# A routed two-layer network on one core: TensorE's products of a turn in another order, the shared weights' split in halves, and weight loads that wait by a table

## The reference

```
gates = xf @ rW + rb
topk_vals, topk_idx = jax.lax.top_k(gates, TOP_K)          # TOP_K = 2 of 8 experts
h = _gelu(jnp.einsum('td,edh->eth', xf, W1) + b1[:, None, :])   # 1024 -> 256
y = jnp.einsum('eth,ehd->etd', h, W2) + b2[:, None, :]          # 256 -> 1024
moe = jnp.einsum('te,etd->td', w, y)
return (shared + moe).reshape(B, L, D)
```

## Time and profile before

| | us |
|---|---|
| median of 3 runs (333.43 to 336.17) | 335.24 |
| the profiled execution, its own time | 334.91 |
| its span, first to last instruction | 333.0 |
| TensorE products busy | 317.9 (95%) |
| TensorE weight loads busy | 274.6 (82%) |
| VectorE busy | 241.2 (72%) |
| ScalarE busy | 188.3 (57%) |
| the loop, from the end of turn 1 to its last product | about 194 to 297.6 |

### The profile page before, as it was taken

One profiled execution on the slowest core, in us unless ns is written; L12 is line 12 of the kernel. 1 busy time (PEld: TensorE's weight loads), 2 busy tenths in 40 slices (PEclk: granted clock), 3 DMA queues, 4 the chain that ended last, 5 costly groups with the idle time before them and its releaser, 6 DMA issues.

```text
span 333.0 us, 6122 instructions
## 1 busy us (share of the span) xinstructions
PE 317.9 (95%) x1994; PEld 274.6 (82%) x1994; DVE 241.2 (72%) x466; ACT 188.3 (57%) x315; POOL 80.2 (24%) x94
## 2 busy tenths in 40 slices
PE   6999999999999999999999999999999999999994
PEld 2889897787799888879989887897788878878874
DVE  2999999976747537845565879768787677480885
ACT  2896999993130323433166897776787678640000
POOL 6641180001010010110213431222144230004840
PEclk9999999999999999999999999999999999999999
DMA  8960013000010145396231595697889972134994
GB/s 246 353 186 2 2 58 116 1 2 17 0 63 3 63 174 190 119 325 261 80 113 65 156 349 190 228 361 296 278 290 338 389 303 112 74 131 159 311 337 180
DMA packets 27014, 57.60 MB, mean 173 GB/s; under 512 B 2735, under 2 KB 16541, under 8 KB 26984
## 3 DMA queue, kind: packets, MB, share of 16 engines
q1 hardware_dynamic: 20458, 33.89, 29.5%
q0 software_dynamic: 3888, 14.16, 12.7%
q10 hardware_dynamic: 2638, 9.17, 7.3%
HBM read 66.25 MB, written 14.03 MB: 241 GB/s over the span
## 4 chain that ended last, share of the span: by engine, by line
PE 48%; ACT 17%; DMA 14%; DVE 8%; issue 6%; POOL 3%; SPq 1%; ACTq 1%; POOLq 1%; DVEq 0%
PE ps L1485 27%; PE ps L1773 6%; PE ps L1609 6%; ACT sw_raw L823 6%; DMA y_acc<-in_x 4%; DMA raw<-in_L_ffn_W 3%; POOL big L664 3%; DMA big<-in_L_ffn_W 3%; DMA big<-yrow,at_i 3%; PE ps L1762 2%; ACT arena_r L758 2%; ACT sw_raw L831 2%; PE ps L1495 2%; DVE xt L1409 2%; DVE arena_r L1389 1%
## 5 line engine op out<-in xcount | busy, mean ns | idle before, releaser
L1485 PE MATMUL ps<-arena_r 128*128 128x512 f32 (+1 forms) x264 | 67.3, 401 | 0.2 <-DVE arena_r L1184 0.2
L1485 PE MATMUL ps<-xt,arena_r 128*128 128x314 f32 (+3 forms) x324 | 60.3, 337 | 0.0
L1485 PE MATMUL ps<-arena_r,xt 128*128 128x286 f32 (+1 forms) x360 | 59.0, 305 | 0.3 <-DVE arena_r L535 0.3
L655 POOL DMA_INDIRECT big<-xrow,tok_i x17 | 34.2, 2011 | 95.9 <-PE ps L1762 76.8
L1485 PEld LDWEIGHTS ps<-arena_r 128*128 128x128 f32 (+1 forms) x264 | 48.0, 188 | 11.0 <-DVE arena_r L1184 0.6
L1485 PEld LDWEIGHTS ps<-xt,arena_r 128*128 128x128 f32 (+1 forms) x324 | 51.2, 187 | 5.5 <-issue 0.2
L1485 PEld LDWEIGHTS ps<-arena_r,xt 128*128 128x128 f32 (+1 forms) x360 | 49.2, 187 | 1.3 <-DVE arena_r L535 0.5
L1389 DVE TENSOR_TENSOR arena_r<-raw,arena_r 128x2048 fp32r<-128x2048 f32 x17 | 38.8, 2284 | 1.6 <-ACT arena_r L985 1.5
L1773 PE MATMUL ps<-big,tile 128*128 x160 | 37.5, 380 | 0.2 <-issue 0.2
L985 ACT ACTIVATE arena_r<-raw 128x2048 fp32r x17 | 32.5, 1910 | 8.0 <-DMA raw<-in_L_ffn_W 4.7
L1773 PEld LDWEIGHTS ps<-big,tile 128*128 128x128 f32 x160 | 29.9, 189 | 5.5 <-issue 1.1
(11 more groups left out here) (234 smaller groups left out, 463.8 us busy)
## 6 DMA issues: line engine op xcount, KB each, us to landing
big<-in_L_ffn_W SPq DMA_DIRECT2D x19, 1024.0 KB, 7.3
raw<-in_L_ffn_W SPq DMA_DIRECT2D x19, 1024.0 KB, 9.9
yrow<-work ACTq DMA_DIRECT2D x17, 512.0 KB, 3.1
raw<-in_L_gnn_W_rel SPq DMA_DIRECT2D x2, 1144.0 KB, 10.8
y_acc<-in_x SPq DMA_DIRECT2D x4, 512.0 KB, 8.2
xrow<-work SPq DMA_DIRECT2D x4, 512.0 KB, 2.9
raw<-in_L_ffn_sW SPq DMA_DIRECT2D x2, 1024.0 KB, 5.8
sw_raw<-in_L_ffn_sW SPq DMA_DIRECT2D x2, 1024.0 KB, 11.8
```

Source lines behind the costliest of these rows:

```text
L655: pool.indirect_dma_start(xg[i % 2], None, xrow, bass.IndirectOffsetOnAxis(tok_i[:, i:i + 1], 0)) \
L1485: ins = pe.matmul(out_ap, a, b, start=start and k == 0, stop=stop and k == n - 1)
```

## The change

Three things change. The table gets a fourth row, `free`, the number of tiles that must be through before tile i's weights may be loaded: i-1 where both tile i and tile i-1 begin an expert, otherwise i-2 (DVE makes it with two more operations). SP reads it into a register and waits on it instead of on i-1; the semaphores that tell of a landed load are three by turns, since a load may now go out before the one two tiles ahead has been counted. Second, in turns 0 to 14 `tile_down(i)` stands before `tile_hidden(i+1)` on TensorE; ACT's and DVE's copies of the down products move ahead of the GELU and of its rest. Turn 15 has the order of before. Third, the split of the first shared network's second weights is made in two halves, behind turns 1 and 2, on ACT and one turn later on DVE.

```diff
+        til_free = til_kept[:, 2:NT]
-        tab = sb("tab", [1, 3, NT], I32)
+        tab = sb("tab", [1, 4, NT], I32)
...
-        s_w1 = [sem(f"s_wone{i}") for i in range(2)]
-        s_w2 = [sem(f"s_wtwo{i}") for i in range(2)]
+        NS_W = 3
+        s_w1 = [sem(f"s_wone{i}") for i in range(NS_W)]
+        s_w2 = [sem(f"s_wtwo{i}") for i in range(NS_W)]
...
-        SW2_AT = (1, NT - 3)
+        SW2_HALVES, SW2_AT = (1, 2), NT - 3
...
                 ring = sp.value_load(tab[0:1, 2, i:i + 1], min_val=0, max_val=1)
+                if i > 2:
+                    free = sp.value_load(tab[0:1, 3, i:i + 1], min_val=1, max_val=NT)
+                elif i == 2:
+                    free = 1
                 if i >= 2:
-                    sp.wait_ge(r_u, i - 1)
+                    sp.wait_ge(r_u, free)
...
                 if i >= 2:
-                    sp.wait_ge(r_w2lo, i - 1)
+                    sp.wait_ge(r_w2lo, free)
...
-                act.wait_ge(s_w2[i % 2], 16 * (i // 2 + 1))
+                act.wait_ge(s_w2[i % NS_W], 16 * (i // NS_W + 1))
...
+                if i != NT - 2:
+                    keep_y_act(i)
                 if i + 1 < NT:
                     tile_gelu(i + 1)
+                if i == NT - 2:
+                    keep_y_act(i)
                 if i + 2 < NT:
                     w2_hi(i + 2, ring_next)
-                keep_y_act(i)
                 store_y(i)
-                if i in SW2_AT:
-                    split_hi(SW2_AT.index(i), True)
+                if i in SW2_HALVES:
+                    half = SW2_HALVES.index(i)
+                    raw_v, hi_v, _ = unit_views(0, True)
+                    act.wait_ge(s_sw2, 16)
+                    act.activation(hi_v[:, half], raw_v[:, half], ACT.Copy).then_inc(s_hi if half else s_sw2h, 1)
+                if i == SW2_AT:
+                    split_hi(1, True)
...
+            v.mark(dve.tensor_tensor(til_free[:, :], til_new[:, 2:NT], til_new[:, 1:NT - 1], ALU.mult))
             step(dve.tensor_tensor_scan(til_run[:, :], ones_f[0:1, :], til_new[:, :], -1.0, ALU.mult, ALU.add))
+            v.mark(dve.tensor_tensor(tab[:, 3, 2:NT], til_free[:, :], iota_t[0:1, 0:NT - 2], ALU.add))
...
+                if i == NT - 2:
                     tile_lo(i + 1)
                 keep_y(i)
-                if i - 1 in SW2_AT:
-                    split_lo(SW2_AT.index(i - 1), True)
+                if i < NT - 2:
+                    tile_lo(i + 1)
+                if i - 1 in SW2_HALVES:
...
-                if i + 1 < NT:
-                    tile_hidden(i + 1)
                 if i == 1:
                     pe.wait_ge(f_g, 4)
+                if i == NT - 2:
+                    tile_hidden(i + 1)
                 tile_down(i)
+                if i < NT - 2:
+                    tile_hidden(i + 1)
```

More of the change, by code:

```diff
@@ L354, in program @@
         s_half = sem("s_halflo")
+        s_sw2h = sem("s_stwohalf")
         s_gd = sem("s_gd")
@@ L494, in _ @@
                 ring = sp.value_load(tab[0:1, 2, i:i + 1], min_val=0, max_val=1)
+                if i > 2:
+                    free = sp.value_load(tab[0:1, 3, i:i + 1], min_val=1, max_val=NT)
+                elif i == 2:
+                    free = 1
                 if i >= 2:
-                    sp.wait_ge(r_u, i - 1)
+                    sp.wait_ge(r_u, free)
                 sp.dma_start(big[:, bass.ds(ring * UNIT, UNIT)].rearrange("p (k n) -> p k n", k=KD),
-                             w1v[bass.ds(e, 1)].rearrange("e p k n -> (e p) k n"), cond=new).then_inc(s_w1[i % 2], 16)
+                             w1v[bass.ds(e, 1)].rearrange("e p k n -> (e p) k n"), cond=new).then_inc(s_w1[i % NS_W], 16)
                 if i >= 2:
-                    sp.wait_ge(r_w2lo, i - 1)
+                    sp.wait_ge(r_w2lo, free)
                 sp.dma_start(raw[:, bass.ds(ring * SLOT, UNIT)].rearrange("p (k n) -> p k n", k=KH),
-                             w2v[bass.ds(e, 1)].rearrange("e p k n -> (e p) k n"), cond=new).then_inc(s_w2[i % 2], 16)
-                if i == SW2_AT[1] - 1:
+                             w2v[bass.ds(e, 1)].rearrange("e p k n -> (e p) k n"), cond=new).then_inc(s_w2[i % NS_W], 16)
+                if i == SW2_AT - 1:
                     load_sw2(1)
@@ L1433, in _ @@
                         w1_lo(i + 2, ring_next)
+                if i == NT - 2:
                     tile_lo(i + 1)
                 keep_y(i)
-                if i - 1 in SW2_AT:
-                    split_lo(SW2_AT.index(i - 1), True)
+                if i < NT - 2:
+                    tile_lo(i + 1)
+                if i - 1 in SW2_HALVES:
+                    half = SW2_HALVES.index(i - 1)
+                    raw_v, hi_v, lo_v = unit_views(0, True)
+                    if half == 0:
+                        dve.wait_ge(s_sw2h, 1)
+                    else:
+                        dve.wait_ge(s_hi, U_SW2 + 3 - NLN)
+                    ins = dve.tensor_tensor(lo_v[:, half], raw_v[:, half], hi_v[:, half].bitcast(F32), ALU.subtract)
+                    if half:
+                        ins.then_inc(s_lo, 1)
+                if i - 1 == SW2_AT:
+                    split_lo(1, True)
                 if i == 6:
```

4 lines of the change are left out of this document (2 added, 2 removed).

## The result

| | before | changed |
|---|---|---|
| median (4 runs each), us | 335.25 | 331.56 |
| lowest to highest | 333.43 to 336.17 | 330.53 to 332.25 |
| the profiled execution, its own time | 334.91 | 331.02 |
| its span | 333.0 | 329.0 |
| first product behind the loop starts | 297.55 | 293.66 |

The ratio is 0.9881 (95% interval 0.9845 to 0.9918). So the kernel became 3.7 us faster, where 1.9 was forecast: the time lies in the range, but near rival B (331.4), not at the forecast, and just beyond the 1% that I had given a chance of 0.20. In a second set of runs the ratio was 0.9893 (0.9868 to 0.9917). An execution more than 1.5% above the fastest of its kernel is left out of every comparison and range here; there were three (337.66 and 338.4 of the kernel before, 336.96 of the one with order and halves).

A forecast was written before the change was run, and what follows sets the result against it. TensorE, busy 95% of the span, was taken to bound the kernel. Loads -2.5, halves -0.40, biases +0.26 and loop's end +0.76 sum to -1.9 us, from 335.24 to 333.3; range 331.0 to 335.9.

The forecast's parts named there:

- rival B: Everything lands: the halves, the biases and the loop's end hide because ACT has more to spare; -3.82, 331.4 us, chance 0.17.
- the whole prize: TensorE's loop, tiles 3 to 15: turns longer than 7.04 us lose 3.82 in all, nearly all that can be won.
- A quiet turn: A loop turn in which nothing is late: 7.04 us on TensorE, claimed to stay so under the new order.
- my table: Predicted start times of TensorE, ACT and DVE steps in a new turn, leaving 0.45 us before the split up products.
- The term of the loads, -2.5: Weight loads at tiles 8 and 13: issued earlier, they win 2.5 of the 2.90 us of stalls.
- The halves, -0.40: Shared weights' split in two halves: wins 0.92 us on DVE, but ACT makes the product 0.26 late, twice.
- the biases, +0.26: Shared biases' rounded part on ACT in turn 5: makes the next product 0.26 us late (0 to 0.5).
- D: The time at which the down products of turn i end, set as zero for the new turn's start times.
- The loop's end, +0.76: Behind turn 14's down products: ACT's last shared split delays tile 16's GELU and down products, 0.76 us (0 to 1.2).
- A: Rival: the loads of tiles 8 and 13 stay late; loads' term -0.2, sum +0.4, 335.7 us, chance 0.17.
- C: Rival, slower: ACT steps pass later, so turns 2 to 14 lose 0.35 to 0.45 each; up to 339.2 us, chance 0.12.

The follow-up runs named there:

- the split doubled: The changed kernel with ACT's split of the last shared weights (turn 14) made twice, one after the other: 332.37 us in 4 runs, ratio 0.9897.
- Eleven added pieces: The changed kernel with one more ACT copy, the length of a half, in each of turns 3 to 13: 331.62 us in 6 runs, ratio 0.991.
- the gap filled: The changed kernel with six shared down products moved into TensorE's 0.52 us wait before tile 16's hidden transposes: 331.07 us in 6 runs, ratio 0.9867.

## Why the prediction was right in its mechanism and half in its size

**Right.** The turn is 7.04 us, the stalls are one shared split and the loads, and nothing before or behind the loop changed its length: the measured difference is the 3.82 that the rows gave as the whole prize. The loads leave a turn earlier (W1 of tile 7 by 8.1 us). ACT waits for the down products before its copy in all 17 turns. The landing times that I chose for W2, 9.6 at tile 8 and 10.2 at tile 13, were measured as 10.0 and 10.2; that they came so near is in part luck, since the same load of tile 13 took at most 9.7 in the changed kernel's second profile and 11.0 with the split doubled. A quiet turn has 0.71 to spare, 0.45 by my table. ACT reads W2 of tile 8 after a short wait, which I had named as a sign of being wrong, and it costs nothing.

**The term of the loads, -2.5, was -2.90.** I had `w2_hi` 0.7 late at tile 13 and let 0.4 of it reach TensorE. It is 0.69 late, and 0.71 is to spare. By my table 0.45 was to spare, which leaves 0.25 of the 0.7; these 0.26 more to spare are what the term lacked, and the 0.15 that I gave beyond it for the next turns did not come either. (My own 6.4 and 2.07 two turns on give 9.7 from issue to need, not the 9.5 that I wrote; in the trace it is 264.19 - 254.63 = 9.56, because `w2_hi` starts at 1.87.) Which part of the change took out the loads was not asked in the prediction; the table does alone.

**The halves, -0.40, were -0.92, and the biases, +0.26, were 0.** The step that failed is "it stands before the copy of the rows, so `w1_hi` ends at 7.45 instead of 6.4". With the half `w1_hi` starts at D + 5.58 (197.50 - 191.92), without it at 5.43 (211.43 - 206.00). My table had ACT full up to the copy, but in each turn with nothing late and no piece it waited 0.7 there (the row of L942 above). Eleven added pieces that cost nothing show it.

**The loop's end, +0.76, was 0.** The same table, one turn on: the split starts at D + 3.67 (287.11 - 283.44), not at 4.4. I wrote that this cost "follows from the order alone" and used it against rival B; it followed from the order and from 0.7 us that were not there. With the split doubled the wait does come, and the loop's end is 1.73 later.

The 0.7 is the distance from my 2.07 + 1.91 + 0.33 = 4.31, rounded up to 4.4, to 3.67, and it has three parts. GELU to `w2_hi` was read as 1.24 from the earlier trace rows, but that `w2_hi` starts 0.34 behind the end of the down products, 221.30, for which the program has it wait. Behind a GELU with nothing else to wait for it is 1.04, and a turn of the kernel before could have told that (its timeline):

```profile
199.13 0.63 ACT L969 ACTIVATE tile<-ps,b_tile 128x128 f32<-128x128 f32 x2
...
200.17 1.90 ACT L985 ACTIVATE arena_r<-raw 128x2048 fp32r x1
```

The issue of a store, 0.33, was added to the row of ACT. In the old order that was right: the store stands directly behind the copy that it sends, and the next activation waits 0.40 behind that copy. In the new order GELU and `w2_hi` stand between the copy and the store, the copy is long done, and the issue lies beside the work. What the issue waits for had changed, and my sum carried its old cost over. No run moves the store alone, so why the issue is free in its new place is read from these rows and not tested. And the next activation comes 1.80 behind `w2_hi`'s start where I counted 1.91. Together 0.20 + 0.33 + 0.11 = 0.64.

**The rivals.** B was right in all three terms, for the reason it gave. A did not happen: with the loads of tiles 7 and 12 out of the way, W2 of tiles 8 and 13 landed 10.0 and 10.2 after its issue, soon enough. Tile 10's W1 left 9.8 behind tile 8's (226.74 against 216.97), not 7.0. The Trainium skill, DMA: Bandwidth & Descriptors, "Issuing engines are not separate DMA queues", says that transfers run on the same engines and interleave. The run that moved only tile 7's loads agrees: the next W2 took 10.1 instead of 11.3. The same page's fit in "Anatomy of one DMA" is stated there for transfers that GpSimd issues, and these are SP's; the estimate from it was 9.2 for tile 13's W2, and the kernels with the table have from at most 8.3 to 11.0, so it is no bound. C did not happen: on the path to `w2_hi` no ACT step came later than the old rows said (the GELU at 0.83, `w2_hi` at 1.87 where I had 2.07).

**What stays open.** Whether W2 lands later under the new order. At tile 8 it took 9.1 and 9.2 in the two kernels with the table and the old order; under the new one 9.8, 10.0 and 10.4 in three executions, and in three more (a piece each turn, the split doubled, the gap filled) it was there when ACT came for it, 9.6 to 10.0 behind the issue. At tile 13 it was at most 8.3 twice in the old order; in the new one 10.2 and 11.0, and four times it was there when ACT came, 9.6 to 9.7 behind the issue. ACT comes later in the new order, so a landing sooner than that does not show. The stores leave 1.0 us earlier in the turn (1.75 behind the end of the down products, where it was 2.77), but nothing was run that moves only them. And each of these is one execution's value.

## What to carry to other kernels

Before a step is put down in a row of start times, ask of every distance between two starts whether a wait lay in it: a distance that held one is an upper bound, and a sum of such distances makes slack look like cost. The same holds for a step that stood directly behind what it waits for: moved away from it, the store's issue cost ACT nothing. A load that is late should be bought time first and made cheaper to wait for second: here one wait that was a tile too strict held the whole of it, and the reordering beside it won nothing that shows once that was gone. And a small gain is sought best where nothing larger varies: without the table the runs of one kernel lay up to 4.7 us apart, and what the halves' 0.92 were worth there no time could show.

## What the runs showed of the hardware

The landing time of the same 1 MB load varies from execution to execution and from kernel to kernel: from at most 8.3 to 12.0 us for W2 of tile 13. The kernel before had 332.53 to 337.27 in 28 runs and 332.75 to 337.36 in 22, and the kernels with the table stayed within 2.1 us in each set of 4 to 6. That the loads make this spread is not shown: fewer runs spread less by themselves, and in one set the kernel before stayed within 2.4 us in 11 runs.

The issue of a transfer by ACT, 0.33 to 0.36 us, can lie beside ACT's work: at 193.66 the issue, at 193.79 the next activation, and the one after that 1.80 later, at 195.59. This is so where what it sends was long done. Directly behind the copy that it sends it did not: in the kernel before the next activation started 0.40 behind the copy's end, at 224.44, with the issue at 224.07 and 0.33 long. At 290.69 it is the same.

A transfer that is conditional and not taken still holds SP's row at its wait: 206.49 in the run that changed tile 7 alone.
